# A two-layer decoder on one core: the reciprocal root between stages by Sqrt on ScalarE and reciprocal plus one Newton step on VectorE, in place of a power on GpSimd

## What is computed

```python
def _layernorm(x, axis=-1, eps=1e-05):
    m = jnp.mean(x, axis=axis, keepdims=True)
    v = jnp.var(x, axis=axis, keepdims=True)
    return (x - m) / jnp.sqrt(v + eps)
...
x = _layernorm(x + _L0_attn_ref(x, ...), axis=-1)          # stage a: cumulative attention and gate
x = _layernorm(x + _L0_xattn_ref(x, ctx_1024, ...), axis=-1)  # stage b: cross attention, 16 heads
x = _layernorm(x + _L0_ffn_ref(x, ...), axis=-1)           # stage m: mixture of 8 experts
x = _layernorm(x + _L1_attn_ref(x, ...), axis=-1)          # stage s: selective scan
x = _layernorm(x + _L1_xattn_ref(x, ctx_1024, ...), axis=-1)  # stage c: cross attention, inner norm
x = _layernorm(x + _L1_ffn_ref(x, ...), axis=-1)           # stage q: quantised feed-forward
```

## Time and profile before

| | before |
|---|---|
| median of 3 runs | 3575.87 us (3572.97 to 3580.39) |
| the profiled execution | 3569.94 us, of which the span is 3568.1 us |
| granted TensorE clock, mean of the span | 0.905 of full speed |
| busy: PE, DVE, POOL, ACT | 2788.9, 2699.4, 1957.8, 1627.7 us |
| stages in the profile (first instruction of each) | b at 274.8, m at 756.0, s at 1285.5, c at 2382.0, q at 3309.3 us |

### The profile page before, as it was taken

The page is one execution under the profiler, slowest core; times in us unless marked ns, Lnnn a source line. Parts: engine busy times, 40 slices in busy tenths (PEclk is TensorE's granted clock), DMA queues, the critical chain, the costliest instruction groups (busy, mean ns, idle before and its releaser), DMA issues. The chain is left out here.

```text
span 3568.1 us, 59422 instructions
## 1 busy us (share of the span) xinstructions
PE 2788.9 (78%) x18120; PEld 1772.7 (50%) x18120; DVE 2699.4 (76%) x4251; ACT 1627.7 (46%) x3050; POOL 1957.8 (55%) x1702
## 2 busy tenths in 40 slices
PE   4767777879899537877777778659999999998455
PEld 2434555546556312332333333238888888886222
DVE  3767888846534329999999999967888878887787
ACT  3535666634222135655655556423333333333565
POOL 1226777747656547777777777743333333333444
PEclk9987999979999869999999999999999999999555
DMA  5701000001155433334333333300000000000000
GB/s 187 330 0 22 18 17 16 13 14 43 42 151 160 123 117 133 129 119 143 130 126 135 131 131 130 130 14 3 3 3 3 3 3 3 3 3 2 9 18 21
DMA packets 136956, 248.05 MB, mean 70 GB/s; under 512 B 50017, under 2 KB 104822, under 8 KB 116226
## 3 DMA queue, kind: packets, MB, share of 16 engines
q1 hardware_dynamic: 121392, 223.49, 18.6%
q0 software_dynamic: 9088, 16.94, 1.4%
q10 hardware_dynamic: 6354, 6.27, 0.6%
HBM read 189.34 MB, written 59.13 MB: 70 GB/s over the span
## 5 line engine op out<-in xcount | busy, mean ns | idle before, releaser
L1741 POOL TENSOR_TENSOR s_drive<-s_du,s_b_sb 128x1024 f32<-128x1024 f32 x256 | 602.0, 2354 | 267.1 <-DVE s_state_ps L1967 266.8
L2080 PE MATMUL s_y_ps<-s_read,w_ident 128*128 128x512 f32 x1024 | 529.7, 648 | 201.6 <-DVE s_read L1981 200.4
L1967 DVE TENSOR_TENSOR_SCAN s_state_ps<-s_decay_ps,s_drive 128x512 f32<-128x512 f32 x512 | 600.3, 1218 | 105.0 <-ACT s_decay_ps L1874 59.6
L1874 ACT ACTIVATE s_decay_ps<-s_delta,neg_rate 128x508 f32<-128x508 f32 x512 | 348.2, 686 | 375.0 <-DVE s_state_ps L1967 374.8
L2080 PEld LDWEIGHTS s_y_ps<-s_read,w_ident 128*128 128x128 f32 x1024 | 193.9, 203 | 516.5 <-DVE s_read L1981 317.5
L2295 ACT ACTIVATE c_pT<-c_turn_ps 77x512 f32<-77x512 f32 x256 | 151.2, 592 | 483.8 <-PE c_turn_ps L2485 483.8
L2264 POOL TENSOR_TENSOR c_p<-c_p,c_norm 128x1232 f32<-128x1232 f32 x64 | 147.0, 2297 | 324.5 <-DVE c_norm L2377 324.5
L1981 DVE TENSOR_TENSOR s_read<-s_state_ps,s_c_sb 128x1024 f32<-128x1024 f32 x256 | 313.6, 1225 | 12.7 <-DVE s_state_ps L1967 1.4
L1360 POOL DMA_INDIRECT m_y_scratch<-e_y,e_index x156 | 152.5, 978 | 92.0 <-DVE e_y L1406 51.0
L685 ACT ACTIVATE b_pT<-b_turn_ps 77x512 f32<-77x512 f32 x256 | 145.4, 591 | 119.1 <-PE b_turn_ps L810 119.1
L619 POOL TENSOR_TENSOR b_p<-b_p,b_top 128x1232 f32<-128x1232 f32 x64 | 143.9, 2248 | 94.9 <-DVE b_top L742 94.9
(11 more groups left out here) (340 smaller groups left out, 6668.0 us busy)
## 6 DMA issues: line engine op xcount, KB each, us to landing
s_b_sb<-s_bc_scratch SPq DMA_DIRECT2D x64, 1024.0 KB, 4.7
s_c_sb<-s_bc_scratch SPq DMA_DIRECT2D x64, 1024.0 KB, 4.7
m_rows_scratch<-fill SPq DMA_DIRECT2D x33, 1040.0 KB, 26.5
e_w<-in_m_we_dram SPq DMA_DIRECT2D x39, 384.0 KB, 3.2
e_xg<-m_rows_scratch SPq DMA_DIRECT2D x39, 260.0 KB, 3.4
k_y<-m_y_scratch SPq DMA_DIRECT2D x32, 256.0 KB, 3.5
x<-in_x_dram SPq DMA_DIRECT2D x16, 256.0 KB, 2.9
out_dram<-q_result SPq DMA_DIRECT2D x16, 256.0 KB, 2.3
```

Source lines behind the costliest of these rows:

```text
L1741: nc.gpsimd.tensor_tensor(drive[:, n % 2, :, :], du[:, s, :, :], b_sb[:, n, :].unsqueeze(1).broadcast_to([128, halves, GT]), ALU.mult).the ...
L1874: nc.scalar.activation(decay[:, m, :, 1:], delta[:, s, m, :].rearrange("p (b t) -> p b t", t=T)[:, :, 1:], ACT.Exp, scale=core.neg_rate[:, ...
L1967: nc.vector.tensor_tensor_scan(state[:, h, :], decay[:, h, :, :].rearrange("p b t -> p (b t)"), drive[:, n % 2, h, :], 0.0, ALU.mult, ALU. ...
L2080: last = nc.tensor.matmul(y_ps[:, m, :], core.ident[:, :], read[:, n % deep, m, :], start=False, stop=(n == states - 1))
```

## The change

`finish_statistics` no longer uses POOL. ACT takes the square root of the scaled variance into a new tile `root`; DVE takes its reciprocal r, and one Newton step r(1.5 - 0.5 v r r) gives `rstd` in three more instructions. DVE's first instructions are reordered: the sum of the spreads goes ahead of the sum of the means, and the halving of the mean moves behind the scaling of the variance.

```diff
-    with nc.sbuf_tensor(f"{name}_gap", [128, B], F32) as gap, nc.Block() as block:
+    with ExitStack() as ctx:
+        gap, root, turn = (ctx.enter_context(nc.sbuf_tensor(f"{name}_{what}", [128, B], F32))
+                           for what in ("gap", "root", "newton"))
+        block = ctx.enter_context(nc.Block())
...
+        @block.scalar
+        def _(act):
+            act.wait_ge(folded, 8 * done + 4)
+            nc.scalar.activation(root[:, :], core.rstd[:, :], ACT.Sqrt).then_inc(rooted, 1)
...
             nc.vector.tensor_tensor(gap[:, :], mean_even, mean_odd, ALU.subtract)
+            nc.vector.tensor_tensor(core.rstd[:, :], spread_even, spread_odd, ALU.add).then_inc(folded, 1)
             nc.vector.tensor_tensor(core.mean[:, :], mean_even, mean_odd, ALU.add)
-            nc.vector.tensor_tensor(core.rstd[:, :], spread_even, spread_odd, ALU.add).then_inc(folded, 1)
-            dve.wait_ge(folded, 4 * done + 1)
-            nc.vector.tensor_scalar(core.mean[:, :], core.mean[:, :], 0.5, None, ALU.mult)
+            dve.wait_ge(folded, 8 * done + 1)
             nc.vector.scalar_tensor_tensor(gap[:, :], gap[:, :], half_n / 2.0, gap[:, :],
                                            ALU.mult, ALU.mult).then_inc(folded, 1)
...
-        @block.gpsimd
-        def _(pool):
-            pool.wait_ge(folded, 4 * done + 4)
-            nc.gpsimd.tensor_tensor(core.rstd[:, :], core.rstd[:, :], core.minus_half[:, 0:B],
-                                    ALU.pow).then_inc(rstd_ready, 1)
-            pool.wait_ge(rstd_ready, done + 1)
+            nc.vector.tensor_scalar(core.mean[:, :], core.mean[:, :], 0.5, None, ALU.mult)
+
+            dve.wait_ge(rooted, done + 1)
+            nc.vector.reciprocal(root[:, :], root[:, :]).then_inc(folded, 1)
+            dve.wait_ge(folded, 8 * done + 5)
+            nc.vector.tensor_tensor(turn[:, :], core.rstd[:, :], root[:, :], ALU.mult).then_inc(folded, 1)
+            dve.wait_ge(folded, 8 * done + 6)
+            nc.vector.scalar_tensor_tensor(turn[:, :], turn[:, :], -0.5, root[:, :],
+                                           ALU.mult, ALU.mult).then_inc(folded, 1)
+            dve.wait_ge(folded, 8 * done + 7)
+            nc.vector.scalar_tensor_tensor(core.rstd[:, :], turn[:, :], 1.5, root[:, :],
+                                           ALU.add, ALU.mult).then_inc(folded, 1)
```

More of the change, by code:

```diff
@@ L121, in finish_statistics @@
     half_n = D // 2
-    with nc.sbuf_tensor(f"{name}_gap", [128, B], F32) as gap, nc.Block() as block:
-        folded, rstd_ready = core.folded, core.rstd_ready
+    with ExitStack() as ctx:
+        gap, root, turn = (ctx.enter_context(nc.sbuf_tensor(f"{name}_{what}", [128, B], F32))
+                           for what in ("gap", "root", "newton"))
+        block = ctx.enter_context(nc.Block())
+        folded, rooted = core.folded, core.rooted
         done = "abmscq".index(name)
@@ L130, in _ @@
             nc.vector.tensor_tensor(gap[:, :], mean_even, mean_odd, ALU.subtract)
+            nc.vector.tensor_tensor(core.rstd[:, :], spread_even, spread_odd, ALU.add).then_inc(folded, 1)
             nc.vector.tensor_tensor(core.mean[:, :], mean_even, mean_odd, ALU.add)
-            nc.vector.tensor_tensor(core.rstd[:, :], spread_even, spread_odd, ALU.add).then_inc(folded, 1)
-            dve.wait_ge(folded, 4 * done + 1)
-            nc.vector.tensor_scalar(core.mean[:, :], core.mean[:, :], 0.5, None, ALU.mult)
+            dve.wait_ge(folded, 8 * done + 1)
             nc.vector.scalar_tensor_tensor(gap[:, :], gap[:, :], half_n / 2.0, gap[:, :],
                                            ALU.mult, ALU.mult).then_inc(folded, 1)
-            dve.wait_ge(folded, 4 * done + 2)
+            dve.wait_ge(folded, 8 * done + 2)
             nc.vector.tensor_tensor(core.rstd[:, :], core.rstd[:, :], gap[:, :], ALU.add).then_inc(folded, 1)
-            dve.wait_ge(folded, 4 * done + 3)
+            dve.wait_ge(folded, 8 * done + 3)
             nc.vector.tensor_scalar(core.rstd[:, :], core.rstd[:, :], 1.0 / D, LN_EPS,
                                     ALU.mult, ALU.add).then_inc(folded, 1)
-        @block.gpsimd
-        def _(pool):
-            pool.wait_ge(folded, 4 * done + 4)
-            nc.gpsimd.tensor_tensor(core.rstd[:, :], core.rstd[:, :], core.minus_half[:, 0:B],
-                                    ALU.pow).then_inc(rstd_ready, 1)
-            pool.wait_ge(rstd_ready, done + 1)
+            nc.vector.tensor_scalar(core.mean[:, :], core.mean[:, :], 0.5, None, ALU.mult)
[9 more added lines that the diff above has]
+                                           ALU.add, ALU.mult).then_inc(folded, 1)
 def leave(dve, nc, core, g, steps, total, stats):
@@ L2985, in build @@
         core.folded = ctx.enter_context(nc.semaphore("folded"))
-        core.rstd_ready = ctx.enter_context(nc.semaphore("rstd_ready"))
+        core.rooted = ctx.enter_context(nc.semaphore("rooted"))
         core.rows_dram = nc.dram_tensor("m_rows_scratch", [FILLS * 128 * FILL_ROWS, ROW], F32, kind="Internal").ap()
```

## The result

| | before | after |
|---|---|---|
| median of 4 runs | 3575.38 us (3572.97 to 3580.39) | 3542.79 us (3537.16 to 3544.80) |
| the profiled execution | 3569.94 us, span 3568.1 | 3537.16 us, span 3535.4 |

The ratio of the runs is 0.9905 (95% interval 0.9887 to 0.9922): 34 us faster, 28 to 40 by the interval. Forecast were 47 us and 3529, with a range up to 3540. The direction held, the size did not: 13.8 us are missing, and the time lies 2.8 us above the range.

The account below looks back on a forecast made before the run. The chain between stages, with POOL's 10.56 us power, was taken as the bound: 9.14 us off the chain plus 0.2 at the barrier, five times, 46.7 us from 3575.9 gives 3529 us, range 3518 to 3540.

Parts of the forecast that it names:

- The joints: The five stretches between stages, from DVE's first fold instruction to the next stage: 9.3 us less each, 46.7 in all.
- Table load at the head of the block: ACT's load for the square root at each boundary: runs at once, takes 1.28 us, hides behind DVE's fold.
- 1.4 us drain: The skill page's cost beside the 1283 ns load: root later by some 1.4 us, five times, saving smaller by about 7.
- The two new loads: ACT table loads ahead of the first exponential in stages b and c: 1.28 us each, fitting into idle time, cost 0.
- whatever leaves it leaves the span: On the chain between stages: barriers leave no second branch, so all time saved there shortens the whole run.
- Behind it nothing moves: Behind the barrier at each boundary: SP's block that raises the next stage's semaphores is unchanged, after 0.2 us less.
- What is freed: In the next stage: POOL's work and stage b's loads start with the barrier, 9.3 us earlier, distance to users unchanged.
- 6 us of clock: Range term for TensorE's clock at the starts of the stages: +-6 us over all stages.
- the four: Rivals: serial table load, clock surviving the gap, clock staying down, and nothing happening (3570 to 3580 us, chance 0.02).
- The serial load: At each boundary, table load or root starts only after DVE's fold: 1.3 to 1.4 us lost each, 3536 to 3538; 0.06.
- The surviving clock: Across the shortened gap s to c, TensorE stays at 2.4 GHz and stages start warm: 3517 to 3527 us; chance 0.05.
- the slower one: TensorE's clock stays down in stage b or m, eating the saving; 3705 us if all of b; chance 0.01.

Follow-up runs that it names:

- root_sc_only: The kernel before with the new finish_statistics only behind stages s and c, the power on POOL kept behind a, b and m; 3638.6 us, ratio 0.9942 to the kernel before.
- before_pad18: The kernel before with 18 one-column memsets on DVE while it waits for the first x; 3563.2 us, ratio 0.9960 to the kernel before.
- after_pad6: The changed kernel with 6 one-column memsets on DVE while it waits for the first x; 3512.5 us, ratio 0.9811 to the kernel before.
- after_shift128: The changed kernel with 114 one-column memsets on DVE while it waits for the first x; 3599.6 us where the kernel before took 3657.0, ratio 0.9850.
- after_pad100: The changed kernel with 100 one-column memsets on DVE while it waits for the first x; 3530.9 us in one run.
- after_same: The changed kernel again, unedited, beside the kernel before on the same chip; 3539.5 us, ratio 0.9899 to the kernel before.
- before_pad12: The kernel before with 12 one-column memsets on DVE while it waits for the first x; 3592.2 us, ratio 1.0057 to the kernel before.
- after_thin_c: The changed kernel with one 1 MB load of C rows in stage s cut to 32 columns of one row, for timing only; 3530.6 us in one run.

## Why the prediction was right in its sum and wrong in the time

**The joints: right.** Table load at the head of the block: forecast to end about 1.26 us after DVE's start, measured 1.25 (260.94 + 1.28 - 260.97). Root at 1.32, measured 1.29; its length 0.27, measured 0.26. Reciprocal 0.55 by the line between 16 and 512 columns, measured 0.553. Newton step 2.22 to 2.96, measured 2.16 to 2.90. From there to `b_shift` 1.97 us, where 2.16 lay between POOL's end and it: 0.19 less for 0.2. Nothing of the 1.4 us drain was seen here either, so the Trainium skill's "ScalarE: Activation LUTs", section "What ACT_TABLE_LOAD costs", is right in its 1283 ns and not borne out in the rest: the root starts 0.04 us behind the load. All in all 47.0 us for 46.7.

**The two new loads: right.** The timeline of the changed kernel, ACT in stage b and in stage c:

```profile
278.78 1.28 ACT L691 ACT_TABLE_LOAD   x1
281.02 1.23 ACT L691 ACTIVATE b_p<-b_p 128x1232 f32<-128x1232 f32 x1 [0.95 <-POOL b_p L631]
...
2371.28 1.28 ACT L2300 ACT_TABLE_LOAD   x1
2374.58 1.23 ACT L2300 ACTIVATE c_p<-c_p 128x1232 f32<-128x1232 f32 x1 [2.02 <-DVE c_p L2380]
```

Of the idle 2.25 and 3.32 us 0.95 and 2.02 are left behind the loads; both exponentials still wait for their own releaser.

**The step that failed** is the sentence at the head of the argument, "whatever leaves it leaves the span", with "Behind it nothing moves" and "What is freed": I let each stage keep its length. I counted the instructions that the change adds to DVE by their time in the chain, and not by what their number does to the place of all later code. The row that carried the missing term was in the trace of before and I had not read it: five waits of 2 us at the top of stage s's loop, four of them under POOL's name. The bound on stage lengths that I did take, 6 us of clock, had the wrong mechanism and was too small; the stalls made stage s 17 us longer. The spans differ by 14 us less than the forecast and not by 17 because stage b came out 3.2 us shorter; that is within its spread (below) and was luck.

**The rivals.** None of the four happened. The serial load is refuted by the rows above. The surviving clock is refuted by the granted clock of the changed kernel: from 2357 to 2359 us, ahead of stage c, it was 0.50, and 0.50 in the first 24 us of stage b as in the earlier trace rows; stages m, c and q kept their lengths to about 1 us. For the slower one the mechanism was wrong, but its form, a stage that loses at its own pace what the joints gain, was that of what came. The clock did its share of noise: stage b was 464 to 478 us long over these profiles, with no edit in it, at a mean granted clock of 0.95 in the shortest (`after`) and of 0.92 in the longest (`root_sc_only`).

## What to carry to other kernels

A chain between two barriers can be priced to 0.1 us from rows of the same kernel, and a power worked out column by column on POOL is worth replacing where it stands alone on such a chain. But adding or removing even a dozen instructions on an engine moves every later loop of that engine; where a loop can touch four packets of its instructions, as the one of 295 can and those of up to 77 cannot, look for waits at its top that recur once a pass, before and after, whatever name they bear, and try a few idle instructions ahead of it. Here six memsets are worth 27 us, more than half of what the change itself brings; with them the kernel takes 3512.5 us, 67.5 under the kernel before (with 50 memsets 3511.7, no real difference). A comparison of two kernels that differ in instruction count can have this error in it until both have been tried at a good place. The two that were, `before_pad18` and `after_pad6`, put the worth of the change at 50.7 us (the joints are 47.0 of it) and not at 33.

## What the runs showed of the hardware that was not expected

- A jump back into a packet of instructions that has to be fetched again cost DVE 1.9 to 2.3 us (`before`, `after_shift128`, `after_pad100`). Where the packet ends within the next two or three instructions, DVE waited for the one behind it too: 5.6 to 6.0 us in all with a 1 MB transfer starting at the same time (`after`, `after_same`, `before_pad12`), 4.1 to 4.6 with that transfer made small (`after_thin_c`).
- A loop of 295 instructions ran without any such wait when it touched three packets of 8 KB, and with one at each jump back when it touched four. With three the queue brought no instruction inside the loop, with four it brought five packets a pass.
- The two branches around an added block of DVE's took no place in this count: 10 memsets with them stood two instructions short of the place of 12, 12 stood right.
- One chip took 3657 us for a kernel that takes 3575 to 3580 on others, and nearly all of it is in stage m. What in it is slower stays open.
